# A new order of work inside each chunk of an edge sort: prefix products, base counts, block residuals and column pieces

## The reference

```python
# x [1250, 512]; src, dst, edge_weight [41250]; layer norms without affine terms
h = relu(layernorm(x))
m = relu(concat(h[src], h[dst]) @ W0.T + b0)          # 41250 messages of 512
x = x + segment_sum(m, src, 1250)
h = relu(layernorm(x))
o = segment_sum((h @ W1.T)[src] * edge_weight, dst, 1250)
x = x + where(o >= 0, o, alpha * o)
```

## Time and profile before

| | before |
|---|---|
| median of 3 runs | 1154.58 us (1152.33 to 1157.19) |
| the profiled execution | 1152.84 us |
| its span, first to last instruction | 1150.9 us |
| mean granted TensorE clock | 0.971 of full speed |
| busy: TensorE, weight load | 92%, 73% |
| busy: VectorE, ScalarE, GpSimd | 84%, 71%, 64% |
| columns placed by TensorE, by scatter | 180, 150 |

### The profile page before, as it was taken

The page is one execution under the profiler, slowest core; times in us unless marked ns, Lnnn a source line. Parts: engine busy times, 40 slices in busy tenths (PEclk is TensorE's granted clock), DMA queues, the critical chain, the costliest instruction groups (busy, mean ns, idle before and its releaser), DMA issues. The chain is left out here.

```text
span 1150.9 us, 22667 instructions
## 1 busy us (share of the span) xinstructions
PE 1059.2 (92%) x5051; PEld 834.8 (73%) x5052; DVE 969.1 (84%) x1780; ACT 822.6 (71%) x1690; POOL 738.2 (64%) x1060
## 2 busy tenths in 40 slices
PE   3388898989799999999999999999999999969997
PEld 3176666766578888888888888888888888847776
DVE  7889898986669999999999999999999999974443
ACT  3766666657578888888888888888888888855210
POOL 5478888778577777777767677777777777650000
PEclk9579999999989999999999999999999999989999
DMA  4000000000000000000000000000000000010011
GB/s 170 27 3 2 3 3 3 3 3 2 17 1 1 0 0 0 0 0 0 0 0 0 0 0 0 0 0 0 0 0 0 0 0 0 0 33 4 9 36 45
DMA packets 9532, 10.52 MB, mean 9 GB/s; under 512 B 5243, under 2 KB 5718, under 8 KB 9499
## 3 DMA queue, kind: packets, MB, share of 16 engines
q1 hardware_dynamic: 4635, 9.78, 2.6%
q0 software_dynamic: 4864, 0.33, 1.6%
HBM read 6.65 MB, written 3.15 MB: 9 GB/s over the span
## 5 line engine op out<-in xcount | busy, mean ns | idle before, releaser
L860 POOL TENSOR_TENSOR M<-M,pair_w 125x125 f32 x432 | 221.0, 512 | 201.2 <-DVE pair_w L1070 161.7
L1084 DVE SCALAR_TENSOR_TENSOR msg_lo<-edge_ps,msg_hi 128x512 fp32r<-128x512 f32 x432 | 294.4, 687 | 58.6 <-ACT msg_hi L1012 52.3
L1012 ACT ACTIVATE msg_hi<-edge_ps 128x512 fp32r<-128x512 f32 x432 | 259.0, 599 | 106.7 <-PE edge_ps L935 106.6
L358 POOL DMA_INDIRECT edge_table<-fields,row_no x150 | 197.3, 1315 | 65.7 <-issue 61.0
L890 PE MATMUL node_ps<-msg_hi,hot_s 128*125 128x512 f32 x432 | 211.0, 489 | 0.2 <-DVE msg_lo L1084 0.2
L599 PE MATMUL psum<-hot_tile,lane_piece 125*128 125x432 f32 x540 | 149.7, 390 | 31.9 <-ACT lane_piece L702 31.1
L702 ACT ACTIVATE lane_piece<-hot_lane,fields 125x128 fp32r<-125x128 bf16 x420 | 134.8, 392 | 60.7 <-DVE hot_lane L436 60.3
L929 PE MATMUL edge_ps<-b_hi,turned_d 125*128 x432 | 174.4, 404 | 1.3 <-issue 1.3
L930 PE MATMUL edge_ps<-b_lo,turned_d 125*128 x432 | 171.1, 396 | 0.0
L891 PE MATMUL node_ps<-msg_lo,hot_s 128*125 128x512 f32 x432 | 170.4, 394 | 0.0
L935 PE MATMUL edge_ps<-a_lo,turned_s 125*128 x432 | 170.3, 394 | 0.0
(11 more groups left out here) (213 smaller groups left out, 1838.0 us busy)
## 6 DMA issues: line engine op xcount, KB each, us to landing
S<-in_x_dram SPq DMA_DIRECT2D x1, 2500.0 KB
out_dram<-result SPq DMA_DIRECT2D x10, 250.0 KB
edge_table<-fields,row_no POOLq DMA_INDIRECT x150
w_in<-in_L_gnn_W_dram SPq DMA_DIRECT2D x1, 2048.0 KB, 11.7
w_in<-in_L_gnn_W_dram SPq DMA_DIRECT2D x1, 1024.0 KB, 5.3
edge_table<-zeros SPq DMA_DIRECT2D x1, 432.0 KB, 31.9
raw<-edge_table SPq DMA_DIRECT2D x1, 432.0 KB, 3.0
src_i<-in_src_dram SPq DMA_DIRECT2D x1, 161.1 KB
```

Of the source, the lines that this page charges most:

```text
L358: pool.indirect_dma_start(table_dram[:, :], bass.IndirectOffsetOnAxis(ap=row_no[:, c:c + 1], axis=0), fields[:, c, 0:TABLE_FIELDS], None). ...
L860: pool.tensor_tensor(part, part, pair_w[h][:, j, 0, 0:BN], ALU.add).then_inc(m_added, 1)
L1012: act.activation(msg_hi[j][:], edge_ps[j][:], ACT.Relu).then_inc(hi_ready, 1)
L1084: dve.scalar_tensor_tensor(out=msg_lo[j][:], in0=edge_ps[j][:], scalar=0.0, in1=msg_hi[j][:].bitcast(F32), op0=ALU.max, op1=ALU.subtract). ...
```

## The change

The file gains lines, so that the same step stands some 3 to 5 lines later in the new one (L434 is L439, L702 is L707, L711 is L716, L599 is L604, L636 is L641).

- `KIND`: of the eight V columns of a chunk (2, 6, 11, 15, 20, 24, 29, 33 among the 36) four become A: 2, 11, 20, 29. That makes 20 columns in the five chunks.
- VectorE: low_of_h at columns 8 and 26 (was 5 and 23); bases at 6 (was 7). Picks stay at 14 to 28. The clearing of planes signals a new semaphore, and the first pick of a chunk waits for it.
- TensorE: products at 7 to 14 and 25 to 32 (was 6 to 13 and 24 to 31); low at 15, 17, 33, 35 (was 14, 16, 32, 34); prefix products at 9 to 23 (was 12 to 26).
- ScalarE: the high copies at 13, 16, 31, 34 (was 12, 15, 30, 33); the low copies stay at 16, 17, 34, 35.

```diff
--- before.py
+++ after.py
@@ -55,7 +55,7 @@
 PICK = 7
 NPICK = -(-NBKT // PICK)
 HCOLS = 11
-KIND = "ADADVDADADAVDADADADADVADADADVDADA" * 2
+KIND = "ADADADADADAVDADADADADAADADADVDADA" * 2
 DMA_AT = [c for c in range(CHUNK) if KIND[c] == "D"]
 PE_AT = [c for c in range(CHUNK) if KIND[c] != "D"]
 NPE = len(PE_AT)
@@ -63,6 +63,8 @@
 DVE_BEFORE = [sum(KIND[c] == "V" for c in PE_AT[:i]) for i in range(NPE + 1)]
 BATCH = 10
 NBATCH = len(DMA_AT) * NCHUNK // BATCH
+
+LOW_AT, BASES_AT, PREFIX_AT, PICK_AT = 8, 6, 9, 14
 UNROLL = 4
 KC = D // P
 OHW = BN + 1
@@ -231,6 +233,7 @@
             rows_in = sem("rows_in")
             hot_made = sem("hot_made")
             prefixed = sem("prefixed")
+            planes_clear = sem("planes_clear")
             picked = sem("picked")
             slot_math = sem("slot_math")
             slots_ready = sem("slots_ready")
@@ -402,6 +405,8 @@
                         dve.wait_ge(prefixed, n + 1)
                         if g > 0:
                             dve.wait_ge(picked, n)
+                        else:
+                            dve.wait_ge(planes_clear, k + 1)
                         dve.copy_predicated(planes[:, 0:nb, :].rearrange("p b c -> p (b c)"),
                                             hot[0:EROWS, g * PICK:g * PICK + nb, :].rearrange("p b c -> p (b c)").bitcast(U16),
                                             psum[0:EROWS, 4 + n % 2, 0:nb * CHUNK]).then_inc(picked, 1)
@@ -480,7 +485,7 @@
                     for s in range(5, NBLK):
                         hot_of_block(0, s)
                     dve.tensor_copy(iota_h[:], iota[0:EROWS, 0:P])
-                    dve.memset(planes[:], 0.0)
+                    dve.memset(planes[:], 0.0).then_inc(planes_clear, 1)
 
                     dve.wait_ge(totals, 1)
                     own(dve.tensor_scalar(zt[:], total_ps, (TILE - 1) / 2, 1.0 / TILE, ALU.add, ALU.mult))
@@ -532,17 +537,17 @@
                                 dve.reciprocal(rstd[0:BN, :], sums[:, 2, :]).then_inc(rstd_ready, 1)
                                 dve.wait_ge(rstd_ready, 1)
                                 dve.tensor_tensor(shift[0:BN, :], neg_mean[0:BN, :], rstd[0:BN, :], ALU.mult).then_inc(rstd_ready, 1)
-                            if i in (5, NPE // 2 + 5):
+                            if i in (LOW_AT, NPE // 2 + LOW_AT):
                                 low_of_h(2 * k + i // (NPE // 2))
                             if k + 1 < NCHUNK:
                                 if i < NBLK:
                                     hot_of_block(k + 1, i)
                                 if i == NBLK:
-                                    dve.memset(planes[:], 0.0)
-                                if i == 7:
+                                    dve.memset(planes[:], 0.0).then_inc(planes_clear, 1)
+                                if i == BASES_AT:
                                     bases(k + 1)
-                                if 14 <= i < 14 + NPICK:
-                                    pick(k + 1, i - 14)
+                                if PICK_AT <= i < PICK_AT + NPICK:
+                                    pick(k + 1, i - PICK_AT)
                                 if i == 30:
                                     slots(k + 1)
                                     dve.wait_ge(slots_ready, k + 2)
@@ -665,15 +670,15 @@
                             for b, at in ((2 * k, 0), (2 * k + 1, NPE // 2)):
                                 if i == at + 1:
                                     turn_h(b)
-                                if at + 6 <= i < at + 6 + 2 * KC:
-                                    product(b, (i - at - 6) // KC, (i - at - 6) % KC)
-                                if i in (at + 14, at + 16):
-                                    low(b, (i - at - 14) // 2)
+                                if at + 7 <= i < at + 7 + 2 * KC:
+                                    product(b, (i - at - 7) // KC, (i - at - 7) % KC)
+                                if i in (at + 15, at + 17):
+                                    low(b, (i - at - 15) // 2)
                             if k + 1 < NCHUNK:
                                 if i < 3:
                                     count(k + 1, range(CHUNK // 3 * i, CHUNK // 3 * (i + 1)))
-                                if 12 <= i < 12 + NPICK:
-                                    prefix(k + 1, i - 12)
+                                if PREFIX_AT <= i < PREFIX_AT + NPICK:
+                                    prefix(k + 1, i - PREFIX_AT)
                             elif i == 6:
 
                                 pe.wait_ge(started_ready, 1)
@@ -761,8 +766,8 @@
                                 if i == at + 3:
                                     act.wait_ge(h_ps, b + 1)
                                     act.copy(h1T[0][:, :, 0:BN], turn_ps).then_inc(hT_hi, 1)
-                                if i in (at + 12, at + 15):
-                                    m = (i - at - 12) // 3
+                                if i in (at + 13, at + 16):
+                                    m = (i - at - 13) // 3
                                     act.wait_ge(ab_ps, b * 2 + m + 1)
                                     out_of_psum(b, m, 0, ab_hi_out)
                                 if i in (at + 16, at + 17):
```

## The result

The changed kernel takes 1173.66 us (median of 4 runs, 1169.67 to 1179.41) against 1155.69 for the kernel before (4 runs). The ratio is **1.0164** (95% interval 1.0122 to 1.0206): slower, by less than 2% but clear of the spread. The forecast of 1161.5 had the sign, but the time lies outside its range of 1152 to 1167. The profiled execution took 1171.55, span 1169.9.

The account below looks back on a forecast made before the run. No engine alone bounds the sort; waits between VectorE, ScalarE and TensorE do. Chunks 1 to 3 +2.65, chunk 0 +1.65, last chunk +3.2 - 0.5 give +7.0 on the median 1154.58: 1161.5 us, range 1152 to 1167.

Parts of the forecast that it names:

- Item 1: Tail of all ten blocks: b_lo waits for the second low product; 0.74 us longer, covering three columns instead of four.
- Item 2: First halves of chunks 0 to 3: counts done at 10.3, products at 15.95; 27.6 us, or 25.05 in chunk 0.
- Item 3: Second halves of chunks 0 to 3: VectorE's wait for prefix products goes, so each half takes 24.5 us.
- the pick wait: VectorE's wait for the first prefix product, 2.95 us in one chunk, 12.9 over four; forecast to go.
- two ends: Second halves: 22.9 us if both queues pass each other no wait, 25.95 as in chunk 0 today.
- two queues: Second halves: ScalarE's queue gives first product at 12.1 and a half of 22.6 us, VectorE's 12.4 and 22.9.
- Item 4: Last chunk, without bases: each half 1.6 us longer, +3.2 together, and the end after it 0.5 shorter.
- Item 5: 20 columns' pieces moved from VectorE to ScalarE: 6.5 us less VectorE work, costed at nothing beyond Item 3.
- Item 6: First pick's wait for cleared planes and the base rows' two DMAs: both costed at nothing.
- Rival (a): Faster: VectorE stays the sort's bound throughout, until scatters stop the gain at 4.4 us, 1150.2; chance 0.12.
- Rival (b): The halves of chunks cancel: second halves at 22.9 us, total +0.6, 1155.2; chance 0.22.
- Rival (c): Slower still: base rows land late or second halves stay at 25.95 us, 1167 to 1170; chance 0.06.

Follow-up runs that it names:

- d1_fill_both: Changed kernel plus unread long TensorE matmuls: three in block tails and three behind place 6, chunks 0 to 3; ratio 1.0062, 1161.48 us.
- d2_pfx10: Kernel before with prefix products from column 10 (was 12) and 20 columns' pieces moved to ScalarE, block steps old; ratio 0.9930, 1146.95 us.

## Why the prediction had the sign and missed the size

**Item 1, the tail: right in its length.** Places 5.0 behind b_hi at the end of a chunk (4.97), 5.2 in the middle of one; ten waits before b_lo of about 1.2, and an end of 3.2 after the last b_hi. Its price of 0.74 a block, 7.4 us in all, was too low: the tail cost some 10 us inside the change and 23 alone in the kernel before.

**Item 2, the first half: this is the step that failed.** "Counts is done at 10.3" took ScalarE as working without a gap from b_lo to counts. It waited there for TensorE, and counts was done at 12.3 to 12.8, because TensorE, dry in the tail for 0.96 and 1.55 us, went on at 1.2 GHz. A part of that wait needed no low clock: the earlier trace rows have ScalarE waiting 0.70 for the count products in the kernel before, at a clock of 1.00, and the item left it out. All three first halves got their products at 18.0 to 18.5 instead of 15.95 (7.0 us in three chunks), and in chunk 2 the dry spell during the bases held the clock down over the product run as well: 14.4 instead of 11.64 (the other two ran 11.4). Together the 9.2 us. With the clock held up by fillers counts came at 10.7 and products at 16.5. The order of bases and low_of_h, and 4.90 + 0.68 for them, was right to 0.4 (177.00 to 182.24 is 5.2). What TensorE waited for last, though, was not low_of_h but the pieces of column 7, which stand behind the bases as well: 1.73 us before the places at 181.79. Chunk 0 was right to 0.3.

The Trainium skill (TensorE: Matmul & The Clock Gate, Part 1: The HAM clock gate) says that the throttled clock is the default state and activity releases it. The trace agrees: the lower clock follows eight of the changed kernel's first nine block tails (not the one at 197.03), and none of the eight tails that have fillers in d1_fill_both. The Trainium skill's same section, for modelling, puts the ramp penalty under 1% of a typical kernel's span; here fillers gave back 1.0% of the kernel, in a stretch that is a fifth of it. The rows ahead of the prediction had the clock at 1.00 in the middle chunks, so it was the change that created the term; item 1 had named the starved TensorE and priced only its idle time.

**Item 3, second halves: right in the number** (24.5 forecast, 24.2 to 25.6): the pick wait fell by 8.1 us, and the four halves are 7.6 shorter. The number was a choice between two ends, and in part luck: its two queues had the first product at 12.1 and 12.4 behind b_hi, and it came at 13.8 to 15.2, which no run takes apart. The 25.6 of chunk 3 stands behind more low clock; with the clock up in d1_fill_both it is 24.1, but that all of it comes from the clock is argued, not shown.

**Item 4, last chunk: undersized**, 2.3 and 2.2 where 1.6 was reckoned; the end as reckoned.

**Item 5: wrong value.** Costed at nothing, the pieces gave 1.7 us alone and some 6 inside the change (0.5%, intervals overlapping). The Trainium skill's rule (Perfetto Trace Analysis, Optimizing Scalar/DVE Operations: move work to ScalarE when VectorE is saturated) had the sign. Its condition is not what decided: the gain was smaller where VectorE was busy 45.78 of 51 us and, as far as the intervals tell, larger where it was busy 40.20 of 52.

**Item 6: right.** No row shows a wait for planes or base rows.

**Rival (a)** did not come. The lock from the Trainium skill that stood beside it (SBUF — State Buffer, Who interferes with whom) could have put 5.6 us on the scatters through 20 more short tensor_scalars. No such effect shows. The scatters' group of the kernel with the pieces alone, against 197.3 and 1315 in the earlier trace rows:

```profile
L361 POOL DMA_INDIRECT edge_table<-fields,row_no x150 | 197.7, 1318 | 63.0 <-issue 61.6 <-DVE row_no L429 1.4
```

0.4 us, not 5.6. It is no clean test of the rule: the run also took 20 of the longer instructions away, and no row shows in which mode the short ones ran. The queue that the rival named did become the bound in d2_pfx10, but its sort ends 6.6 us earlier, not 4.4: besides the waits for row numbers the scatters lost some of their stretching (194.8 us for 150, where it was 197.3), which the rival had mentioned. **Rival (b)**, halves that cancel, did not come: second halves stayed at 24.1 to 24.9 even with the clock up in d1_fill_both, where it needed 22.9. **Rival (c)** had nearly the size (1167 to 1170) but another mechanism: base rows were not late, and second halves fell below 25.95.

Two sums of the prediction are off by a little, and nothing hangs on them: 10.3, 4.90 and 0.68 add up to 15.88, not 15.95, and three quarters of 0.60 with 0.06 are 0.51, not 0.52.

## What to carry to other kernels

Where a change makes TensorE run dry for a microsecond or two in a place where it did not, price not only the gap but the work behind it at half the clock, and follow who waits for that work: here about 12 of 18 us were this. Test it by filling the gap with a few long matmuls that nobody reads; if the kernel gets faster with work added and the granted clock is up, the clock is the cost. If it doesn't, as with the short fillers here, the test says nothing. Change the order of such a schedule one number at a time, since the parts don't add: two steps that cost 23 and 25 us alone cost 26 together, and the best version kept only the pieces and two of the three columns by which the prefix products moved.

## What the runs showed of the hardware that was not expected

With fillers of 80 columns, 16 to a block, the last 22 of a chunk's 66 counting matmuls came in groups of 4 to 13 with 0.28 to 0.48 us of issue between, in chunks 1 to 3; with fillers of 432 columns they did not. Why is open.
